# One 4 MB input load per half of the tokens, and a stashed residual read back from memory, in place of small input loads and a residual kept in SBUF

## The chip, the cores and the metric

The kernel runs on 8 cores of one Trainium2 chip. Each core computes its own share of the tokens, with no exchange between cores. The metric is the device time of the slowest core in microseconds (us).

## The reference

One "sandwich" layer over x of shape (4, 2048, 2048), in float32:

```python
x = feat_patch
# --- layer 0 (sandwich) ---
x = x + layernorm(mamba_like_block(layernorm(x)))      # the "attn" part
x = x + layernorm(ffn_with_moe(layernorm(x)))          # the "ffn" part
```

The attn part normalises again, projects 2048 channels to 96, applies a convolution of width 3, a selective scan over time with 16 states per channel, projects 96 back to 2048 and adds its own input:

```python
x = layer_norm(feat_patch, ln_w, ln_b)
x = x @ in_proj_W.T
...
y = ssm(x, x_proj_W, dt_proj_W, dt_proj_b, A_log, D_param)
out = y @ out_proj_W.T
return out + residual
```

The ffn part is a gated MLP of inner width 8192, plus a routed MLP of width 1024 that is scaled by the weights of a top-2 router.

## The kernel before, in words

**Layout.** A core owns 1024 tokens. The data lie transposed: 2048 channels as KC = 16 tiles of 128 partitions, tokens along the free dimension, worked through in halves of 512 (the loop variable is `hc`, the offset `off = 512 * hc`). A tile of 128 x 512 float32 has 256 KB. `x3` is the view of the core's input `xT` as (partition, tile, token).

**Stages in order of time.** The mixer (in-projection, convolution, scan; `xcb` holds the input as bf16, loaded by GpSimd's queue in chunks of 16 tiles x 512 tokens), then stage O (out-projection, residuals, two layer norms; from 443 to 786 us), the router, the routed MLP, the gate and up projections ("gu", 64 blocks), the down projection and the epilogue, which reads the stashed residual again.

**The order of the work.** Each engine runs its instructions in the order in which the program lists them. The class `Sched` gives each operation its semaphore waits: `reads`, `writes` and `waits` become waits for the tokens of earlier operations, a tile's resource (`Res`) holds its last writer and its readers. `S.dma("sync", ...)` issues a DMA from SP, `S.dma("scalar", ...)` from ScalarE's instruction stream (so a wait of such a DMA holds up ScalarE's later instructions), `S.dma("gpsimd", ...)` from GpSimd's. `S.fence()` makes the next instruction of every engine wait for all that was issued so far. `CW` is the list of the constants' loads, which nearly every TensorE operation waits for, too (they landed in the first 22 us).

**Stage O**, for each half `hc`, in this order:

1. *The out-projection loop* over 16 tiles `mc`. SP loads the tile of the input (L830, buffers `xld`, two of them). TensorE multiplies (L836, L838) into a bank of PSUM. VectorE multiplies the input tile by the row of reciprocal deviations (L844, `t_s`) and adds the bank (L847, `t_mr`) into `mr_sb`. ScalarE makes two casts of it, a copy and a square (L775, L777, in `stats_tile`), and TensorE sums them over the channels (L779, L784). TensorE runs in order, so the product of tile `mc + 1` stands behind the sums of tile `mc`.
2. *The rows*: seven small operations on 1 x 512 between ScalarE and VectorE (L793 to L805), and `bcast` (L811 on TensorE, L814 on ScalarE), which spreads a row over 128 partitions, into `bc_a` and `bc_b`.
3. *The residual loop* over 16 tiles `k`. SP loads the input tile again (L862, buffers `xld2`, two of them). VectorE multiplies in place (L866, `tx1`), GpSimd adds (L870, `tx2`), VectorE adds the input tile and writes the result to its own slice of `x2res` (L874, `tx3`). ScalarE issues the store of this tile to `x2_st` in HBM (L878) and makes the two casts (L885, L888); TensorE sums them (L891, L897).
4. *The rows again* (L906 to L922); the last operation is L922 (`tG`). The two results are kept in `rows4`. Then `bcast` twice.
5. *The normalising loop* over 16 tiles `k`: VectorE multiplies `x2res` by `bc_a` into `x2t` (L929, `tz1`, two buffers) and adds `bc_b` into `z4_sb` as bf16 (L932, `tz2`). `z4_sb` is what all later matmuls read.

After the second half the router's matmuls (L952) wait for the last L932.

**Memory.** SBUF is laid out by hand in regions B1, B2 and B3. `mr_sb` (32 KB per partition) lies in B1 over the mixer's tiles, `x2res` (32 KB) in the upper part of B2, `z4_sb` (32 KB) in B3 over `xcb`.

Of the kernel before, what the change touches and what calls it, by code (L numbers as in the profile page):

```python
# [206 lines left out]
def build_program(debug_taps=()):  # L207
# [112 lines left out]
    mr_sb = at("s_mr", (128, 16 * 512), F32, nc.lookup_mloc(xp_all.tensor).addr)  # L320
    assert (nc.lookup_mloc(rowsA.tensor).addr
            >= nc.lookup_mloc(mr_sb.tensor).addr + 32 * 1024), "mr overlaps rows"
    xld = [at(f"s_xld{i}", (128, 512), F32, RW0 + 2048 * i) for i in range(2)]
    xld2 = [at(f"s_xld2{i}", (128, 512), F32, WB0 + 2048 * i) for i in range(2)]
# [18 lines left out]
    sel8_sb = atb2("s_sel8", (8, 8 * 128), F32)  # L343
    cmb8 = atb2("s_cmb8", (8, 128), F32)
    lgt_sb = atb2("s_lgt", (8, 1024), F32)
    lgt_tm = atb2("s_lgttm", (128, 64), F32)
    rt_m1 = atb2("s_rtm1", (128, 8), F32)
    rt_t = atb2("s_rtt", (128, 8), F32)
    rt_t2 = atb2("s_rtt2", (128, 8), F32)
    comb_tm = atb2("s_combtm", (128, 8), F32)  # L350
    outTbf = atb2("s_outTb", (96, 2048), BF16)
    y_f = atb2("s_yf", (96, 1024), F32)
    y_bf = atb2("s_ybf", (96, 1024), BF16)
    rows4 = atb2("s_rows4", (1, 4 * 512), F32)
    cast_bf = [at(f"s_castb{i}", (128, 512), BF16, WB0 + 4096 + 1024 * i) for i in range(2)]
    cast_bf2 = [at(f"s_castb2{i}", (128, 512), BF16, WB0 + 6144 + 1024 * i) for i in range(2)]
    x2t = [at(f"s_x2t{i}", (128, 512), F32, WB0 + 8192 + 2048 * i) for i in range(2)]
    bc_b2 = at("s_bcb2", (128, 512), F32, WB0 + 12288)
    o2[0] = max(o2[0], B2 + 32 * 1024)
    M_SPILL0 = o2[0]  # L360
# [1014 lines left out]
```

How the kernel before makes its waits and increments, by code:

```python
        def run(e, emit=emit, wl=wl, inc=(inc_sem, inc_by), ph=ph, eng=eng):  # L66
            n0 = e.bass.n_instructions() if hasattr(e, "bass") else None
            for s, v in wl:
                e.wait_ge(_SEMS[s], v)
            inst = emit(e)
            inst.then_inc(_SEMS[inc[0]], inc[1])
            n1 = e.bass.n_instructions() if n0 is not None else None
            self.dbg_map[eng].append((n1 - n0 if n0 is not None else 1 + len(wl), ph))
# [133 lines left out]
def build_program(debug_taps=()):  # L207
# [1095 lines left out]
    final_waits = {}  # L1303
    for (s, v, _) in out_toks:
        final_waits[s] = max(final_waits.get(s, 0), v)
    fw = list(final_waits.items())
    def final_op(e, fw=fw):
        for s, v in fw:
            e.wait_ge(_SEMS[s], v)
        return e.nop()
    S.cnt["s_sy"] = S.cnt.get("s_sy", 0) + 1
    S.ops.append(("sync", lambda e: final_op(e).then_inc(_SEMS["s_sy"], 1)))
    with nc.Block() as block:
        @block.sync
```

## Time and profile before

| what | value |
|---|---|
| median of 3 runs | 2717.59 us (2714.5 to 2926.98) |
| the profiled execution's own time | 2718.68 us |
| its span (first to last instruction, core 2, the slowest) | 2717.1 us |
| spans of the 8 cores | 2701.4 to 2717.1 us |
| TensorE busy | 1920.2 us (71%) |
| VectorE, ScalarE, GpSimd busy | 394.6, 466.7, 355.5 us |
| stage O, from the fence to the last L932 | 443.3 to 785.6 us |
| router and routed MLP; gu; down; epilogue | to 1050; to 1940; to 2540; to the end |

The profile is of one execution on the slowest core, and its own time is 1.6 us over its span and 1.1 us over the median. Times are microseconds from the span's start; L12 is line 12 of the kernel. PE is TensorE (PEld its weight loads), DVE VectorE, ACT ScalarE, POOL GpSimd, SP SyncE; ACTq and SPq are the streams that issue DMAs. TensorE's granted clock is printed as a share of 2.4 GHz.

### The profile page before, as it was taken

To read this page: it belongs to the slowest core of one execution; us is meant where nothing else is said; L and a number is where in the kernel's file an instruction comes from. 1 tells how busy PE (TensorE), PEld (TensorE's weight loads), DVE (VectorE), ACT (ScalarE), POOL (GpSimd) and SP (SyncE) were. 2 spreads that over 40 slices of the span, in tenths; PEclk is the share of its full clock that TensorE was granted. 3 is DMA by queue.
4 is the path that set the end of the run, shared out by engine and by line. 5 is a ranking of instruction groups with operands and counts; after the bars stand their busy time and mean duration, and the time that the engine had idled before them with its cause. 6 is when DMAs were issued, how large, how long until landed. Compare 5 with 4: busy or idle time off the path is not lost.

```text
span 2717.1 us, 26955 instructions; the slowest of 8 cores (2701.4 to 2717.1 us)
## 1 busy us (share of the span) xinstructions
PE 1920.2 (71%) x7579; PEld 780.8 (29%) x7719; DVE 394.6 (15%) x589; ACT 466.7 (17%) x802; POOL 355.5 (13%) x400
## 2 busy tenths in 40 slices
PE   4444544434327967999999999999788898888200
PEld 2111110000003423444444444444333333333000
DVE  0553343253341100000000000000000000000222
ACT  3333211222311121111111111111100000000100
POOL 1000000020201201222222222222100000000122
PEclk8555555555558998999999999999899899999555
DMA  7220001131422354444444434344444334443233
GB/s 114 44 32 0 0 0 32 55 109 51 113 47 37 58 135 97 78 78 78 78 78 78 76 74 74 74 76 77 78 94 93 71 84 93 93 93 70 108 139 131
DMA packets 68011, 203.24 MB, mean 75 GB/s; under 512 B 7900, under 2 KB 18269, under 8 KB 63782
## 3 DMA queue, kind: packets, MB, share of 16 engines
q0 software_dynamic: 38608, 124.49, 26.4%
q1 hardware_dynamic: 15446, 35.07, 4.3%
q10 hardware_dynamic: 13824, 41.95, 4.2%
q8 instruction: 78, 1.28, 0.2%
q14 instruction: 55, 0.45, 0.1%
HBM read 292.41 MB, written 33.55 MB: 120 GB/s over the span
## 4 chain that ended last, share of the span: by engine, by line
PE 65%; DVE 11%; DMA 9%; issue 7%; ACT 4%; POOL 3%; DVEq 1%; SPq 0%; ACTq 0%; POOLq 0%
PE pb L1122 16%; PE pb L1131 16%; PE pb L1179 5%; PE pb L1176 4%; PE pb L1194 4%; PE pb L1191 4%; DMA s_epf<-f_stash 3%; DMA s_xld<-xT 2%; PE pb L1037 2%; PE pb L1046 2%; DVE s_xs L738 2%; PE pb L749 2%; DMA s_rdbuf<-Wrd 2%; POOL s_mr L870 1%; PE pb L1079 1%
## 5 line engine op out<-in xcount | busy, mean ns | idle before, releaser
L1122 PE MATMUL pb<-s_z,s_gbuf 128*128 128x512 bf16 x2007 | 461.5, 380 | 15.1 <-issue 12.9
L1131 PE MATMUL pb<-s_z,s_ubuf 128*128 128x512 bf16 x2007 | 459.9, 379 | 2.2
L1122 PEld LDWEIGHTS pb<-s_z,s_gbuf 128*128 128x128 bf16 x2048 | 200.8, 98 | 256.0 <-issue 15.6
L1131 PEld LDWEIGHTS pb<-s_z,s_ubuf 128*128 128x128 bf16 x2048 | 200.3, 98 | 241.7
L1208 DVE TENSOR_TENSOR s_fstg<-pb,s_frbuf 128x512 f32<-128x512 f32 x32 | 20.6, 686 | 1552.7 <-PE pb L1194 1552.7
L1143 POOL TENSOR_TENSOR s_h<-s_gs,s_us 128x512 bf16<-128x512 bf16 x128 | 147.1, 1150 | 678.6 <-ACT s_us L1140 678.6
L1176 PE MATMUL pb<-s_h,s_dbuf 128*128 128x512 bf16 x490 | 200.5, 409 | 18.0 <-issue 17.8
L1179 PE MATMUL pb<-s_h,s_dbuf 128*128 128x512 bf16 x512 | 208.7, 408 | 1.8 <-issue 0.4
L1194 PE MATMUL pb<-s_h,s_dbuf 128*128 128x512 bf16 x512 | 199.2, 389 | 1.1
L1191 PE MATMUL pb<-s_h,s_dbuf 128*128 128x512 bf16 x492 | 191.6, 389 | 4.1 <-PE pb L1179 4.1
L1137 ACT ACTIVATE s_gs<-pb 128x512 bf16<-128x512 f32 x128 | 76.5, 598 | 380.3 <-PE pb L1122 362.6
L1140 ACT ACTIVATE s_us<-pb 128x512 bf16<-128x512 f32 x128 | 76.5, 598 | 365.5 <-PE pb L1131 365.5
L870 POOL TENSOR_TENSOR s_mr<-s_mr,s_bcb 128x512 f32<-128x512 f32 x32 | 40.5, 1265 | 556.2 <-ACT s_bcb L814 501.3
L1216 ACT ACTIVATE s_fbf<-s_fstg 128x512 bf16<-128x512 f32 x32 | 20.1, 630 | 540.2 <-DVE s_fstg L1208 538.5
L749 PE MATMUL pb<-s_dA,s_selR 128*96 128x512 f32 x48 | 47.8, 1100 | 81.9 <-DVE s_dA L746 81.9
L1156 POOL DMA_DIRECT2D s_dbuf<-Wd x32 | 17.1, 533 | 529.3 <-PE pb L1179 314.7
L1079 PE MATMUL pb<-s_rh,s_rdbuf 128*128 128x512 bf16 x251 | 63.5, 410 | 30.7 <-DMA s_rdbuf<-Wrd 28.8
L1176 PEld LDWEIGHTS pb<-s_h,s_dbuf 128*128 128x128 bf16 x512 | 53.3, 104 | 93.2 <-issue 43.6
L779 PE MATMUL pb<-s_castb,s_o128b 128*1 128x512 bf16 x32 | 18.7, 584 | 77.2 <-ACT s_castb L775 77.2
L1179 PEld LDWEIGHTS pb<-s_h,s_dbuf 128*128 128x128 bf16 x512 | 53.0, 104 | 67.6 <-issue 18.0
L1191 PEld LDWEIGHTS pb<-s_h,s_dbuf 128*128 128x128 bf16 x512 | 51.0, 100 | 73.7 <-issue 26.0
L1194 PEld LDWEIGHTS pb<-s_h,s_dbuf 128*128 128x128 bf16 x512 | 51.0, 100 | 61.7 <-issue 13.7
(192 smaller groups left out, 1470.0 us busy)
## 6 DMA issues: line engine op xcount, KB each, us to landing
s_gbuf<-Wg POOLq DMA_DIRECT2D x64, 512.0 KB, 6.2
s_ubuf<-Wu POOLq DMA_DIRECT2D x64, 512.0 KB, 8.2
s_dbuf<-Wd POOLq DMA_DIRECT2D x32, 1024.0 KB, 9.0
s_xld<-xT SPq DMA_DIRECT2D x64, 256.0 KB, 2.9
s_xcb<-xT POOLq DMA_DIRECT2D x5, 2048.0 KB, 15.1
x_stash<-s_x2res ACTq DMA_DIRECT2D x32, 256.0 KB, 3.7
fr_stash<-s_frstg ACTq DMA_DIRECT2D x16, 512.0 KB, 5.7
s_frbuf<-fr_stash ACTq DMA_DIRECT2D x16, 512.0 KB, 8.7
```

The source lines that it names most:

```text
L749: tj8 = S.op("tensor", lambda e, j=j, jb=jb: e.matmul(pb[2][0:96, :], selR_sb[:, 96 * j:96 * (j + 1)], prod_b[jb][:], start=(j == 0), stop ...
L870: tx2 = S.op("gpsimd", lambda e, k=k: e.tensor_add(mr_sb[:, 512 * k:512 * (k + 1)], mr_sb[:, 512 * k:512 * (k + 1)], bc_b[:, :]), reads=[r ...
L1079: i = e.matmul(pb[bank][:, :], rdbuf[db][:, 128 * ikr:128 * (ikr + 1)], r_h_sb[:, 1024 * ikr + hof:1024 * ikr + hof + 512], start=(ikr == ...
L1122: i2 = e.matmul(pb[bg][:, :], gbuf[ib][:, 128 * k:128 * (k + 1)], z4_sb[:, 1024 * k + hof:1024 * k + hof + 512], start=(k == 0), stop=(k = ...
L1131: i2 = e.matmul(pb[bu][:, :], ubuf[ib][:, 128 * k:128 * (k + 1)], z4_sb[:, 1024 * k + hof:1024 * k + hof + 512], start=(k == 0), stop=(k = ...
L1137: tsl = S.op("scalar", lambda e, half=half, bg=bg: e.activation(gs_t[half][:], pb[bg][:, :], AF.Silu), reads=[r_pb[bg]], writes=[r_gs[half ...
L1140: tuc = S.op("scalar", lambda e, half=half, bu=bu: e.activation(us_t[half][:], pb[bu][:, :], AF.Copy), reads=[r_pb[bu]], writes=[r_us[half ...
L1143: S.op("gpsimd", lambda e, i=i, hof=hof, half=half: e.tensor_mul(h_all[:, 1024 * i + hof:1024 * i + hof + 512], gs_t[half][:], us_t[half][:]),
L1176: e.matmul(pb[b0][:, :], dbuf[0][:, 128 * ik:128 * (ik + 1)], h_all[:, 1024 * ik:1024 * ik + 512], start=(ik == 0), stop=False)
L1179: i2 = e.matmul(pb[b1][:, :], dbuf[0][:, 128 * ik:128 * (ik + 1)], h_all[:, 1024 * ik + 512:1024 * (ik + 1)], start=(ik == 0), stop=False)
L1191: e.matmul(pb[b0][:, :], dbuf[1][:, 128 * (ik - 32):128 * (ik - 31)], h_all[:, 1024 * ik:1024 * ik + 512], start=False, stop=(ik == NI - 1))
L1194: i2 = e.matmul(pb[b1][:, :], dbuf[1][:, 128 * (ik - 32):128 * (ik - 31)], h_all[:, 1024 * ik + 512:1024 * (ik + 1)], start=False, stop=(i ...
```

## The change

It replaces the way in which stage O gets its input tiles and keeps its result:

- One load of 16 tiles x 512 tokens (4 MB) per half, from SP, into a new `x_half`, at the top of the half. It replaces the 16 loads of L830 and the 16 of L862. `x_half` lies where `mr_sb` lay; `mr_sb` moves to B3, into the space of `z4_sb`. The second half's load writes what the first half's loops read, so it waits for their last reader.
- `x2res` is gone. The residual loop writes `x2t[k % 2]` and stores it to `x2_st` from there, so it also waits until the store and the casts of tile `k - 2` have read that buffer.
- Because `mr_sb` now lies over `z4_sb`, the normalising loops of both halves run after the second half's residual loop, behind a new `S.fence()`. They read each tile back from `x2_st` into `x2t[k % 3]` (three buffers), even tiles from ScalarE's stream, odd ones from SP's, and work in place.
- Small tiles get other addresses in B2.

The core of the diff:

```diff
+    x_half = at("s_xhalf", (128, 16 * 512), F32,
+                nc.lookup_mloc(xp_all.tensor).addr)
...
-    xld = [at(f"s_xld{i}", (128, 512), F32, RW0 + 2048 * i) for i in range(2)]
-    xld2 = [at(f"s_xld2{i}", (128, 512), F32, WB0 + 2048 * i) for i in range(2)]
...
+    x2t = [atb2(f"s_x2t{i}", (128, 512), F32) for i in range(3)]
+    mr_sb = at("s_mr", (128, 16 * 512), F32, B3)
-    x2res = at("s_x2res", (128, 16 * 512), F32, B2 + 32 * 1024)
...
     for hc in range(2):
         off = 512 * hc
+        t_xh = S.dma("sync", lambda e, off=off: e.dma_start(
+                         out=xh3[:, :, :], in_=x3[:, :, 1024 + off:1024 + off + 512]),
+                     writes=[r_xhalf])
         for mc in range(KC):
-            t_xl = S.dma("sync", lambda e, mc=mc, kk=kk, off=off: e.dma_start(
-                             out=xld[kk][:],
-                             in_=x3[:, mc, 1024 + off:1024 + off + 512]),
-                         writes=[r_xld[kk]])
...
         for k in range(KC):
             kk = k % 2
-            t_x2l = S.dma("sync", lambda e, k=k, kk=kk, off=off: e.dma_start(
-                              out=xld2[kk][:],
-                              in_=x3[:, k, 1024 + off:1024 + off + 512]),
-                          writes=[r_xld2[kk]])
...
             tx3 = S.op("vector", lambda e, k=k, kk=kk: e.tensor_add(
-                           x2res[:, 512 * k:512 * (k + 1)],
-                           mr_sb[:, 512 * k:512 * (k + 1)], xld2[kk][:]),
-                       reads=[r_mr, r_xld2[kk]], writes=[r_x2r[k]], waits=[tx2, t_x2l])
+                           x2t[kk][:], mr_sb[:, 512 * k:512 * (k + 1)],
+                           x_half[:, 512 * k:512 * (k + 1)]),
+                       reads=[r_mr, r_xhalf], writes=[r_x2t[kk]], waits=[tx2, t_xh])
...
-        t_r4b = bcast(bc_a, r_bca, row4(s_r4), r_rows4[s_r4], [tF], 3)
-        t_nm4b = bcast(bc_b, r_bcb, row4(s_nm4), r_rows4[s_nm4], [tG], 4)
+        ln4_toks.append((tF, tG))
+
+    S.fence()
+    for hc in range(2):
+        off = 512 * hc
+        s_r4, s_nm4 = 2 * hc, 2 * hc + 1
+        t_r4b = bcast(bc_a, r_bca, rows4[:, 512 * s_r4:512 * (s_r4 + 1)],
+                      r_rows4[s_r4], [ln4_toks[hc][0]], 3)
+        t_nm4b = bcast(bc_b, r_bcb, rows4[:, 512 * s_nm4:512 * (s_nm4 + 1)],
+                       r_rows4[s_nm4], [ln4_toks[hc][1]], 4)
         for k in range(KC):
-            kk = k % 2
-            tz1 = S.op("vector", lambda e, k=k, kk=kk: e.tensor_mul(
-                           x2t[kk][:], x2res[:, 512 * k:512 * (k + 1)], bc_a[:, :]),
-                       reads=[r_x2r[k], r_bca], writes=[r_x2t[kk]], waits=[t_r4b])
+            kk = k % 3
+            trl = S.dma("scalar" if k % 2 == 0 else "sync",
+                        lambda e, k=k, kk=kk, off=off: e.dma_start(
+                            out=x2t[kk][:], in_=x2_st[k, :, off:off + 512]),
+                        writes=[r_x2t[kk]], waits=[r_x2st[k]])
+            tz1 = S.op("vector", lambda e, kk=kk: e.tensor_mul(
+                           x2t[kk][:], x2t[kk][:], bc_a[:, :]),
+                       reads=[r_bca], writes=[r_x2t[kk]], waits=[trl, t_r4b])
```

The order on VectorE at the turn from the first half to the second, before (line numbers are those of each kernel; `s_rows_115` is `rows4`, `s_x2t` the two buffers, `s_z_144` is `z4_sb`):

```order
L874 TENSOR_TENSOR s_x2res<-s_mr,s_xld_95 128x512
L912 TENSOR_TENSOR s_rows<-s_rows 1x512
L914 TENSOR_TENSOR s_rows<-s_rows 1x512
L922 SCALAR_TENSOR_TENSOR s_rows_115<-s_rows,s_rows_115 1x512
L929 TENSOR_TENSOR s_x2t_120<-s_x2res,s_bca 128x512
L932 TENSOR_TENSOR s_z_144<-s_x2t_120,s_bcb 128x512
```

and the same place after the change:

```order
L862 TENSOR_TENSOR s_x2t_135<-s_mr,s_xhalf 128x512
L899 TENSOR_TENSOR s_rows<-s_rows 1x512
L901 TENSOR_TENSOR s_rows<-s_rows 1x512
L909 SCALAR_TENSOR_TENSOR s_rows_129<-s_rows,s_rows_129 1x512
L836 TENSOR_TENSOR s_bcb<-s_xhalf,s_bca 128x512
L839 TENSOR_TENSOR s_mr<-pb,s_bcb 128x512
```

The 32 instructions of the first half's normalising loop left this place; the second half's first product with `x_half` follows directly on the rows.

The order on ScalarE at the end of stage O, before (L957 is the router's):

```order
L906 ACTIVATE s_rows<-pb 1x512
L909 ACTIVATE s_rows<-pb 1x512
L916 ACTIVATE s_rows<-s_rows 1x512
L918 ACTIVATE s_rows_115<-s_rows 1x512
L814 ACTIVATE s_bca<-pb 128x512
L814 ACTIVATE s_bcb<-pb 128x512
L957 ACTIVATE s_lgt<-pb 8x512 x2
```

and after, up to the turn between the two normalising loops (`s_x2t_134`, `_135` and `_136` are the three buffers; the odd tiles' loads stand on SP):

```order
L905 ACTIVATE s_rows_129<-s_rows 1x512
L810 ACTIVATE s_bca<-pb 128x512
L810 ACTIVATE s_bcb<-pb 128x512
L925 DMA s_x2t_134<-x_stash 128x512
L925 DMA s_x2t_136<-x_stash 128x512
...
L925 DMA s_x2t_136<-x_stash 128x512
L810 ACTIVATE s_bca<-pb 128x512
L810 ACTIVATE s_bcb<-pb 128x512
L925 DMA s_x2t_134<-x_stash 128x512
L925 DMA s_x2t_136<-x_stash 128x512
```

ScalarE's eight loads of each half stand behind both of that half's broadcasts.

## Rows read from the trace of the kernel before

**Rows 1.** Busy time in one stretch, the first half's residual loop.

```profile
core 2: us, PE busy (x) PEld busy (x) DVE busy (x) ACT busy (x) POOL busy (x), PEclk, DMA share, GB/s
...
532.60:582.90 50.30, 18.39 (x31) 2.38 (x30) 22.16 (x32) 17.84 (x31) 20.23 (x16) 0.50 0.57 163
```

**Rows 2.** The chain that ended last, window 458 to 470: start, us, what.

```profile
458.90 2.43 DMA s_xld<-xT
...
461.34 0.58 PE pb L836
```

**Rows 3.** Timeline, tiles 13 and 15 of the first out-projection loop: start, us [idle before].

```profile
511.95 0.58 PE L836 MATMUL pb<-s_ybf,s_outTb 96*128 96x512 bf16 x1 [0.63 <-DMA s_xld<-xT]
...
522.07 0.58 PE L836 MATMUL pb<-s_ybf,s_outTb 96*128 96x512 bf16 x1 [0.64 <-PE pb L784]
```

**Rows 4.** Waits in window 425:790: us in total, times, longest.

```profile
DVE s_mr L847 <- PE pb L838: 114.1, 30, 4.1
...
DVE s_x2res L874 <- POOL s_mr L870: 50.6, 32, 2.5
```

**Rows 5.** Timeline at the start of stage O.

```profile
442.53 0.63 ACT L764 ACTIVATE s_ybf<-s_yf 96x512 bf16<-96x512 f32 x1 [5.97 <-DVE s_yf L760]
443.33 36.01 SPq L830 DMA_DIRECT2D s_xld<-xT  x10
...
443.51 2.04 PE L811 MATMUL pb<-s_r1own,s_o1x 1*128 1x512 f32 x2 [1.93 <-ACT s_ybf L764]
...
446.51 0.69 DVE L844 TENSOR_TENSOR s_bcb<-s_xld,s_bca 128x512 f32<-128x512 f32 x1 [4.08 <-DMA s_xld<-xT]
```

**Rows 6.** DMA in 443:447, 40 slices of 0.1 us: the first two 256 KB loads.

```profile
GB/s 0 0 0 0 0 0 0 0 0 0 0 0 0 143 102 82 143 225 143 369 389 369 369 389 410 369 369 389 410 307 226 21 20 0 0 0 0 0 0 0
```

**Rows 7.** DMA in 55:75, 0.5 us slices: one load of `xcb`, bytes written.

```profile
GB/s 0 0 0 0 0 0 0 0 0 0 0 4 66 57 147 207 205 199 199 207 203 213 207 205 211 207 203 172 188 195 166 184 152 115 156 113 25 8 0 0
```

**Rows 8.** DMA to landing: all `xcb` loads; L830 alone; L862 alone; L878's stores; the epilogue's reads of the stash.

```profile
DMA to landing us min/median/max: 14.8/15.1/32.0
...
DMA to landing us min/median/max: 2.5/2.6/3.9
...
DMA to landing us min/median/max: 2.7/3.5/5.0
...
DMA to landing us min/median/max: 2.0/3.7/5.2
...
DMA to landing us min/median/max: 4.4/4.8/6.6
```

**Rows 9.** Timeline, from the first residual loop to the second half.

```profile
582.16 0.69 DVE L874 TENSOR_TENSOR s_x2res<-s_mr,s_xld 128x512 f32<-128x512 f32 x1 [1.51 <-POOL s_mr L870]
...
588.92 0.68 DVE L922 SCALAR_TENSOR_TENSOR s_rows<-s_rows,s_rows 1x512 f32<-1x512 f32 x1 [1.55 <-ACT s_rows L918]
...
594.34 0.68 DVE L929 TENSOR_TENSOR s_x2t<-s_x2res,s_bca 128x512 f32<-128x512 f32 x1
...
595.12 0.69 DVE L932 TENSOR_TENSOR s_z<-s_x2t,s_bcb 128x512 bf16<-128x512 f32 x1
595.73 0.69 DVE L929 TENSOR_TENSOR s_x2t<-s_x2res,s_bca 128x512 f32<-128x512 f32 x1
...
615.54 0.69 DVE L844 TENSOR_TENSOR s_bcb<-s_xld,s_bca 128x512 f32<-128x512 f32 x1
```

**Rows 10.** Timeline, end of stage O.

```profile
759.10 0.68 DVE L922 SCALAR_TENSOR_TENSOR s_rows<-s_rows,s_rows 1x512 f32<-1x512 f32 x1 [1.54 <-ACT s_rows L918]
759.25 3.75 PE L811 MATMUL pb<-s_rows,s_o1x 1*128 1x512 f32 x4 [3.23 <-ACT s_rows L918]
...
763.15 0.60 ACT L814 ACTIVATE s_bcb<-pb 128x512 f32<-128x512 f32 x1 [1.16 <-PE pb L811]
...
784.91 0.69 DVE L932 TENSOR_TENSOR s_z<-s_x2t,s_bcb 128x512 bf16<-128x512 f32 x1
785.96 6.01 PE L952 MATMUL pb<-s_z,s_routerTb 128*8 128x512 bf16 x16 [22.96 <-DVE s_z L932]
```

More of the change, by code:

```diff
@@ L319, in build_program @@
                   nc.lookup_mloc(dA_b[0].tensor).addr)
[L320 removed]
+    x_half = at("s_xhalf", (128, 16 * 512), F32,
+                nc.lookup_mloc(xp_all.tensor).addr)
     assert (nc.lookup_mloc(rowsA.tensor).addr
[L322 to L324 removed]
+            >= nc.lookup_mloc(x_half.tensor).addr + 32 * 1024), "x_half overlaps rows"
     rh_tmp = at("s_rhtmp", (128, 1024), BF16, B1)
@@ L342, in build_program @@
     routerTbf = atb2("s_routerTb", (128, 128), BF16)
[L343 to L360, printed above, removed]
     xprojTbf = atb2("s_xprojTb", (96, 38), BF16)
@@ L379, in build_program @@
     selR_sb = atb2("s_selR", (128, 12 * 96), F32)
+    y_f = atb2("s_yf", (96, 1024), F32)
+    y_bf = atb2("s_ybf", (96, 1024), BF16)
+    lgt_sb = atb2("s_lgt", (8, 1024), F32)
+    lgt_tm = atb2("s_lgttm", (128, 64), F32)
+    rt_m1 = atb2("s_rtm1", (128, 8), F32)
+    rt_t = atb2("s_rtt", (128, 8), F32)
+    rt_t2 = atb2("s_rtt2", (128, 8), F32)
+    rows4 = atb2("s_rows4", (1, 4 * 512), F32)
+    cast_bf = [atb2(f"s_castb{i}", (128, 512), BF16) for i in range(2)]
+    cast_bf2 = [atb2(f"s_castb2{i}", (128, 512), BF16) for i in range(2)]
+    x2t = [atb2(f"s_x2t{i}", (128, 512), F32) for i in range(3)]
+    bc_b2 = atb2("s_bcb2", (128, 512), F32)
+    comb_tm = atb2("s_combtm", (128, 8), F32)
     B3 = B2 + 64 * 1024
@@ L843, in build_program @@
             r_bcb_i = r_bcb if mc % 2 == 0 else r_bcb2
-            t_s = S.op("vector", lambda e, kk=kk, bcb_i=bcb_i: e.tensor_mul(
-                           bcb_i[:, :], xld[kk][:], bc_a[:, :]),
-                       reads=[r_xld[kk], r_bca], writes=[r_bcb_i], waits=[t_xl, t_r1b])
+            t_s = S.op("vector", lambda e, mc=mc, bcb_i=bcb_i: e.tensor_mul(
+                           bcb_i[:, :], x_half[:, 512 * mc:512 * (mc + 1)], bc_a[:, :]),
+                       reads=[r_xhalf, r_bca], writes=[r_bcb_i], waits=[t_xh, t_r1b])
             t_mr = S.op("vector", lambda e, mc=mc, bank=bank, bcb_i=bcb_i: e.tensor_add(
@@ L874, in build_program @@
             tx3 = S.op("vector", lambda e, k=k, kk=kk: e.tensor_add(
[L875 to L882 removed]
+                           x2t[kk][:], mr_sb[:, 512 * k:512 * (k + 1)],
+                           x_half[:, 512 * k:512 * (k + 1)]),
+                       reads=[r_mr, r_xhalf], writes=[r_x2t[kk]], waits=[tx2, t_xh])
+            tst = S.dma("scalar", lambda e, k=k, kk=kk, off=off: e.dma_start(
+                            out=x2_st[k, :, off:off + 512], in_=x2t[kk][:]),
+                        reads=[r_x2t[kk]], waits=[tx3])
+            r_x2st[k] = tst if hc == 0 else tst
             cb4 = cast_bf if k % 2 == 0 else cast_bf2
             rc4 = r_cast if k % 2 == 0 else r_cast2
[L885 to L890 removed]
+            tca = S.op("scalar", lambda e, kk=kk, cb4=cb4: e.activation(
+                           cb4[0][:], x2t[kk][:], AF.Copy),
+                       reads=[r_x2t[kk]], writes=[rc4[0]], waits=[tx3])
+            tcb = S.op("scalar", lambda e, kk=kk, cb4=cb4: e.activation(
+                           cb4[1][:], x2t[kk][:], AF.Square),
+                       reads=[r_x2t[kk]], writes=[rc4[1]], waits=[tx3])
             ts1 = S.op("tensor", lambda e, k=k, cb4=cb4: e.matmul(
```

22 lines of the change are left out of this document (5 added, 17 removed).

## The prediction

> **What bounds the kernel now.** I read the page first: TensorE is busy 71% of the span, and the change touches none of the stages where it is. Stage O, from 443.3 to 785.6 us, is the only place it touches, so all views were read there. In it TensorE's granted clock is 0.50 (1.2 GHz) and DVE is busy less than half of the residual loop: 22.16 of 50.30 us [rows 1]. No engine is full there; each loop runs at the length of a chain of small operations.
>
> In the out-projection loop the waits show a circle: DVE's L847 waits for TensorE's L838 in 30 of 32 cases, 114.1 us in total [rows 4]; it releases ScalarE's cast, and that TensorE's sums, behind which the next product stands. One turn takes (522.07 - 511.95) / 2 = 5.06 us [rows 3]. The chain view tells something else: it runs through the load of `xld`, 2.43 us in each turn, which ends just as L836 starts [rows 2]. This is the place to doubt. At tile 13 L836 starts after 0.63 us idle, put down to the load; at tile 15, when this loop has no load left to wait for, the idle time is 0.64 us and the turn no shorter [rows 3]. L836 reads no `xld`, and the load lands in that gap by coincidence. So I take the small loads as hidden, apart from the first.
>
> In the residual loop DVE waits for GpSimd in all 32 cases [rows 4]; its turn is 50.3 / 16 = 3.14 us [rows 1] and does not depend on the load of L862 either. The normalising loop is DVE alone: 1.40 us a tile ((784.91 - 763.15 - 0.77) / 15, from the first L932 just behind the broadcast) [rows 10], the same as from one L929 to the next, 595.73 - 594.34 = 1.39 [rows 9].
>
> **Part A, the first 4 MB load.** Before, the first product L844 starts at 446.51, 3.18 us after SP's first issue [rows 5]. After, it waits until the whole of `x_half` has landed. No row shows a 4 MB load on SP's queue. Two things are near: the two first `xld` loads began to move at 444.3, 1.0 us after the issue, and from 444.9 on ran at 369 to 410 GB/s, so that they count as started at 1.5 us [rows 5, 6]; and a load of `xcb`, which reads the same 4 MB with the same runs of 2 KB, takes 14.8 us at least, 15.1 at the median and 32.0 at most [rows 8], moving data for about 12.5 us [rows 7] (it writes bf16, so what is read is double the 205 GB/s shown). From below: 1.5 + 4.19 MB / 410 GB/s + 0.3 for the end = 12.0 us. From above: 32.0 us, when two such loads and the constants ran at once. The value I take is 14.0 us, just below the quiet `xcb` load, since SP's loads start moving a little sooner. L844 then starts at 443.33 + 14.0 + 0.1 = 457.4: **+10.9 us**. Nothing hides it; only one broadcast stands beside it.
>
> The row first: the two loads ran at 369 to 410 GB/s, with all cores at work [rows 6]. The Trainium skill (DMA: Bandwidth & Descriptors, Anatomy of one DMA) gives 2.0 us plus bytes / 436 GB/s, which would be 11.6 us for 4 MB, and the sum below would be 4.8 us smaller; its section Bandwidth puts about 358 GB/s per core when both cores of an HBM domain stream, so 13.7 us by the same form. I stay with the rows.
>
> **Part B, the turn between the halves.** The second load can go out when the last L874 has read `x_half`: 582.16 + 0.69 + 0.08 = 582.93 [rows 9]; it lands at 596.9. Beside it run the rows up to 588.92 + 0.68 = 589.6, so some 7.3 us stay open. L844 starts at 597.0 instead of 615.54 [rows 9], because the 32 normalising instructions are no longer between: **-18.5 us**. From there to the last L922 nothing is changed.
>
> The residual loop gets a new wait: `tx3` of tile k must wait for the store of tile k-2. Two turns are 6.28 us, less its own 0.69; the store lands after 3.7 us, 5.2 at most [rows 8], so even the slowest has 0.3 us to spare. Queued behind a late `tx3` would be DVE's next `tx1`, then GpSimd and the casts. Cost 0, at most 1 us. The casts read the buffer within 2 us and don't matter. The new addresses I cost at nothing.
>
> **Part C, the normalising loops at the end.** Before, from the end of the last L922 (759.78) to the end of the last L932 (785.60) there are 25.8 us [rows 10]. After:
> - The fence holds TensorE's broadcast until L922 is done. At the fence ahead of stage O it starts 443.51 - 443.16 = 0.35 us after the last operation [rows 5]: 760.13 instead of 759.25. `bc_b` is then ready 0.88 us later than now, at 764.63 [rows 10].
> - ScalarE's loads stand behind this broadcast. Tile 0 is issued at 764.73. Its landing time: 2.5 to 3.9 us for quiet loads of this size, median 2.6, 3.5 beside stores; 4.4 to 6.6 for the double size in the epilogue [rows 8]. I take 2.8, near the quiet ones, because no store runs by then but two loads overlap. First product at 767.61.
> - Each buffer goes round in 0.78 + 0.69 (L929 start to L932 end [rows 9]) + 0.08 + 2.8 + 0.08 = 4.43 us, for three buffers 1.48 us a tile, against 1.40 of DVE. So the loads bound it, barely. First half's end: 767.61 + 15 x 1.48 + 1.47 = 791.28.
> - At the turn tile 0 needs `bc_b`'s broadcast (0.17 + 0.60), the issue (0.10) and a landing (2.88), bare: 795.03. Second half's end: 818.70.
>
> That is 818.70 - 785.60 = **+33.1 us**. The first half's loop came back (22.4), and 10.7 are added by the fence, the two bare landings and the longer turn. The router follows as before.
>
> **The sum.** +10.9 - 18.5 + 33.1 = +25.5 us. The profiled execution took 2718.68 us, so 2744.2; against the median of the runs, 1.1 us lower, 2743.1. I say 2743.5. The bytes moved are about the same: 64 loads of 256 KB before, 2 of 4 MB and 32 of 256 KB after. No stage after 786 us is touched; two runs of before differ by 3 us.
>
> **The rivals.**
> 1. *The chain view is right, and the small loads did set the turn.* For it: rows 2, in nearly every turn. Then with the input in SBUF each of 32 turns of the out-projection loop loses the load's part. L836 could start when L784 is through, 0.63 us earlier [rows 3]: -20.2 us, and a sum of +5 us, 2724. For the end to come out not slower than before, the turn would have to lose over 25.5 / 32 = 0.8 us; if it fell by the whole 2.43 us of the load it would be -78, and 2666, faster by 1.9%. Against it: tiles 13 to 15, and that the wait is named at an instruction which doesn't read the tile.
> 2. *The 4 MB load is slow.* Place: the top of each half, and it counts twice, since the second one is bare beyond 7 us. Every us over 14.0 costs 2. At the longest `xcb` landing, 32.0 us [rows 8], it is +36, so 2780, slower by 2.3%; from 28.5 us on it is over 2%. For it: all cores start it at the same moment, and the queue's longest loads in the trace are far smaller. Against it: the quiet `xcb` loads are made at the same moment on all cores too and take 15.
> 3. *The reloads are slow.* With 3.5 us a landing the tile takes 1.71 us, +8.3 in all, 2752; with 4.8, 2.14 us, +24, so 2768. For it: each waits for a buffer, so nothing averages it out. Against it: 256 KB per 1.48 us are 177 GB/s, less than half of what rows 6 show.
> 4. *The reloads cost nothing.* With 2.6 us a landing or less DVE's 1.40 us is the bound: -3, 2741.
>
> **How the numbers follow.** My own case with rival 4: 0.70. Rival 3: 0.12, mostly its near end. Rival 2: 0.10, most of it at 18 to 24 us, 2751 to 2763; over 28.5 us 0.03. Rival 1: 0.08, of which 0.02 for a gain over 2%. My case alone spans 2737 (load 12.0 us, turn 1.40) to 2750. The range for 8 in 10 goes from 2736 to 2762. 2% (54 us) is about what a measurement of this kernel can tell from no change: faster 0.02, same 0.93, slower 0.05 (rival 2 at its far end, or 2 and 3 together).
>
> **What would show it.** In the profile after: the first L836 (the old L844) some 14 us after SP's issue; that DVE instruction again some 14 us after the last `tx3` of the first half; turns of 5.06 and 3.14 us unchanged; two runs of 16 products with `x2t` at 1.4 to 1.5 us a tile; the last one some 25 us later than 785.6. I am wrong if the out-projection turn is shorter than 4.9 us, if `x_half` lands after more than 18 us, if `tx3` waits for a store, or if the stages after the router take another time than now.

## The result, and the profile after

The changed kernel takes 2750.91 us at the median of 10 runs (2743.08 to 2996.43); the kernel before, run beside it, 2715.57 us (2713.88 to 2926.98). The ratio is 1.0126, with a 95% interval of 1.0109 to 1.0143, so 34.2 us longer (29.6 to 38.8). The forecast was 2743.5 us in a range of 2736 to 2762, and "within 2%": the time lies in the range and in that case, but the sum of +25.5 us was 9 us short. The disturbed runs at the upper ends are left out of this ratio and all that follow, though not out of the medians.

The profiled execution after the change took 2751.17 us. The spans of the cores after the change (us from first to last instruction, mean granted clock of TensorE):

```profile
core 0: 2732.7 us, clock 0.806
...
core 2: 2733.9 us, clock 0.805
...
core 4: 2749.6 us, clock 0.804
...
die 0 (median of its cores): 2737.1 us, clock 0.806
die 1 (median of its cores): 2738.3 us, clock 0.806
```

The two dies agree in span and clock, but the single cores differ by 17 us. I had read the trace of before on core 2 alone; after the change core 4 is the slowest. So the table is a mean over the eight cores, each read from its own timeline. "To first product" runs from SP's first issue in stage O to the first product of the input tile (the old L844); "first half, rest" goes on to the start of the half's last row operation, L922 (now L909); the two columns after it are counted from the end of such an operation, so its own 0.7 us stands in none of the four, but in stage O; the last column is all that stands behind stage O. Us:

| kernel | to first product | first half, rest | first half's end to second half's end | from there to the last L932 (L931) | stage O | behind it |
|---|---|---|---|---|---|---|
| before | 3.2 | 142.4 | 170.2 | 25.8 | 342.3 | 1921.0 |
| after | 16.1 | 142.4 | 154.1 | 61.2 | 374.6 | 1917.8 |
| forecast of the difference | +10.9 | 0 | -18.5 | +33.1 | +25.5 | 0 |
| measured difference (before rounding) | +12.9 | +0.1 | -16.0 | +35.4 | +32.4 | -3.2 |

Each of the three parts has the sign and nearly the size that was forecast, and each was 2.0 to 2.5 us too favourable. What lies behind stage O is not longer; that it is 3.2 us shorter says little, since there the eight cores of the kernel before alone differ by 18 us (1913.1 to 1931.5). By core, stage O grew by 28.2 us (core 2) to 35.9 (core 1).

The loads and the stores on core 4, in the view of the DMA issues (output and input, queue, count, KB each, median us from issue to landing):

```profile
s_xhalf<-xT SPq DMA_DIRECT2D x2, 4096.0 KB, 17.0
x_stash<-s_x2t ACTq DMA_DIRECT2D x32, 256.0 KB, 2.0
...
s_x2t<-x_stash SPq DMA_DIRECT2D x16, 256.0 KB, 2.9
s_x2t<-x_stash ACTq DMA_DIRECT2D x16, 256.0 KB, 3.0
```

The 4 MB load takes 17.0 us here where 14.0 were forecast (the trace has one landing of the two, that of the first load); a reload takes 2.9 to 3.0 where 2.8 were. The stores land in 2.0 us, against 3.7 before [rows 8], when loads ran beside them, so `tx3` had 1.7 us more to spare than was reckoned.

The waits on core 4 in the window 425:850 (who waits for whom: us in total, times, longest):

```profile
DVE s_mr L839 <- PE pb L830: 113.4, 30, 4.1
...
DVE s_x2t L862 <- POOL s_mr L858: 50.9, 32, 2.5
...
DVE s_bcb L836 <- DMA s_xhalf<-xT: 30.1, 2, 18.4
...
DVE s_x2t L928 <- DMA s_x2t<-x_stash: 13.6, 9, 7.9
```

The first two answer to [rows 4] and have not moved (114.1 and 50.6 before): the loops wait for the same things as long as ever. The third is new, two waits and 30.1 us: it is what the large load leaves open at the top of each half. The fourth is the bare landing behind the fence (7.9 us), the one at the turn between the two normalising loops (3.4) and small gaps beside them. VectorE waits for a store nowhere in this window, so the new wait of the residual loop cost nothing.

The timeline of core 4 from the start of stage O to its end (start, us, engine, line, what, and in brackets the idle time before and what ended it):

```profile
445.94 0.40 SPq L820 DMA_DIRECT2D s_xhalf<-xT  x1
...
463.44 0.69 DVE L836 TENSOR_TENSOR s_bcb<-s_xhalf,s_bca 128x512 f32<-128x512 f32 x1 [18.41 <-DMA s_xhalf<-xT]
...
599.06 0.69 DVE L862 TENSOR_TENSOR s_x2t<-s_mr,s_xhalf 128x512 f32<-128x512 f32 x1 [1.51 <-POOL s_mr L858]
599.83 0.38 SPq L820 DMA_DIRECT2D s_xhalf<-xT  x1
...
605.87 0.68 DVE L909 SCALAR_TENSOR_TENSOR s_rows<-s_rows,s_rows 1x512 f32<-1x512 f32 x1 [1.55 <-ACT s_rows L905]
...
618.26 0.69 DVE L836 TENSOR_TENSOR s_bcb<-s_xhalf,s_bca 128x512 f32<-128x512 f32 x1 [11.71 <-DMA s_xhalf<-xT]
...
760.95 0.68 DVE L909 SCALAR_TENSOR_TENSOR s_rows<-s_rows,s_rows 1x512 f32<-1x512 f32 x1 [1.54 <-ACT s_rows L905]
761.99 7.16 PE L807 MATMUL pb<-s_rows,s_o1x 1*128 1x512 f32 x8 [4.12 <-DVE s_rows L909]
...
769.52 0.69 DVE L928 TENSOR_TENSOR s_x2t<-s_x2t,s_bca 128x512 f32<-128x512 f32 x1 [7.90 <-DMA s_x2t<-x_stash]
...
793.97 0.69 DVE L931 TENSOR_TENSOR s_z<-s_x2t,s_bcb 128x512 bf16<-128x512 f32 x1
...
798.04 0.69 DVE L928 TENSOR_TENSOR s_x2t<-s_x2t,s_bca 128x512 f32<-128x512 f32 x1 [3.39 <-DMA s_x2t<-x_stash]
...
821.82 0.69 DVE L931 TENSOR_TENSOR s_z<-s_x2t,s_bcb 128x512 bf16<-128x512 f32 x1
822.87 3.57 PE L950 MATMUL pb<-s_z,s_routerTb 128*8 128x512 bf16 x8 [53.72 <-DVE s_z L931]
```

It is read as pairs. The first product waits from the issue at 445.94 to 463.44. The second load goes out 0.08 us after the last read of `x_half` (599.06 + 0.69 = 599.75), and the next product comes 18.43 us after that issue; of these the rows hide some 6.7 us (to 605.87 + 0.68), and 11.71 are bare. From the end of the second half's rows (760.95 + 0.68 = 761.63) it is 7.89 us to the first normalising product, from there 25.14 to the end of the first loop's last L931, 3.38 to the next product and 24.47 to the end of the last L931, 822.51. The router (L950) follows 0.36 us later, as before [rows 10].

### The profile page after: what moved, and what is told of

Its sections match the earlier page's. It is cut to its first block, busy times and chain, and to the rows that moved or that the text cites. A ratio compares the mean times of both kernels' runs of the same rounds, so it can differ in the third digit from the quotient of the medians.

```text
span 2749.6 us, 26926 instructions; the slowest of 8 cores (2732.7 to 2749.6 us)
## 1 busy us (share of the span) xinstructions
PE 1913.5 (70%) x7579; PEld 779.6 (28%) x7719; DVE 396.2 (14%) x589; ACT 466.2 (17%) x802; POOL 355.5 (13%) x400
## 4 chain that ended last, share of the span: by engine, by line
PE 65%; DVE 11%; DMA 9%; issue 7%; ACT 4%; POOL 3%; DVEq 0%; SPq 0%; ACTq 0%; POOLq 0%
PE pb L1120 16%; PE pb L1129 16%; PE pb L1177 5%; PE pb L1174 4%; PE pb L1192 4%; PE pb L1189 4%; DMA s_epf<-f_stash 3%; PE pb L1035 2%; PE pb L1044 2%; DVE s_xs L734 2%; PE pb L745 2%; DMA s_rdbuf<-Wrd 2%; POOL s_mr L858 1%; PE pb L1077 1%; DMA s_xhalf<-xT 1%
## 5 line engine op out<-in xcount | busy, mean ns | idle before, releaser
L1174 PE MATMUL pb<-s_h,s_dbuf 128*128 128x512 bf16 x490 | 201.2, 411 | 15.6 <-issue 15.2
L1177 PE MATMUL pb<-s_h,s_dbuf 128*128 128x512 bf16 x512 | 209.4, 409 | 1.8 <-issue 0.4
L1192 PE MATMUL pb<-s_h,s_dbuf 128*128 128x512 bf16 x512 | 194.0, 379 | 1.1
L1189 PE MATMUL pb<-s_h,s_dbuf 128*128 128x512 bf16 x492 | 186.4, 379 | 4.2 <-PE pb L1177 4.2
L1189 PEld LDWEIGHTS pb<-s_h,s_dbuf 128*128 128x128 bf16 x512 | 50.0, 98 | 70.2 <-issue 11.6
```

The lines of the kernel that those rows point to most:

```text
L1174: e.matmul(pb[b0][:, :], dbuf[0][:, 128 * ik:128 * (ik + 1)], h_all[:, 1024 * ik:1024 * ik + 512], start=(ik == 0), stop=False)
L1177: i2 = e.matmul(pb[b1][:, :], dbuf[0][:, 128 * ik:128 * (ik + 1)], h_all[:, 1024 * ik + 512:1024 * (ik + 1)], start=(ik == 0), stop=False)
L1189: e.matmul(pb[b0][:, :], dbuf[1][:, 128 * (ik - 32):128 * (ik - 31)], h_all[:, 1024 * ik:1024 * ik + 512], start=False, stop=(ik == NI - 1))
L1192: i2 = e.matmul(pb[b1][:, :], dbuf[1][:, 128 * (ik - 32):128 * (ik - 31)], h_all[:, 1024 * ik + 512:1024 * (ik + 1)], start=False, stop=(i ...
```

## The experiments

Nine kernels ran, one of them twice. e1, e2 and e3 each take away one part of what the change brought; e4 and e6 put parts of it into the kernel before; e5 cuts the large load of the changed kernel in two; e7 (run again as e7b), e8 and e9 shorten the loops' turns themselves. Each ratio is to the kernel before, run beside it in the same series; the medians of different series are not to be compared (the kernel before had 2715.6, 2730.1, 2719.3 and 2733.2 us in the four); stage O and its stretches are means over the eight cores of the profiled execution.

### The input by tiles instead of in one load (e1)

`x_half` stays, but is filled by 16 loads of 256 KB, each with its own resource, so that the product of tile `m` waits for tile `m` alone.

```diff
-        t_xh = S.dma("sync", lambda e, off=off: e.dma_start(
-                         out=xh3[:, :, :], in_=x3[:, :, 1024 + off:1024 + off + 512]),
-                     writes=[r_xhalf])
+        for m in range(KC):
+            t_xh[m] = S.dma("sync", lambda e, m=m, off=off: e.dma_start(
+                                out=x_half[:, 512 * m:512 * (m + 1)],
+                                in_=x3[:, m, 1024 + off:1024 + off + 512]),
+                            writes=[r_xh[m]])
```

> The changed kernel with x_half loaded as 16 loads of 256 KB with their own waits instead of one of 4 MB. My theory: the first product starts about 3.2 us after the first issue (16.1 on average over the cores now), -13 us; in the second half it follows the rows at once, -9 us (16.1 us of landing less the 7 us of rows beside it). So some 22 us less than the changed kernel, 2729. Rival (the loads' bytes cost time however they are cut, by contention with the stores): under 10 us less, with stores that land in 3.7 us again and tx3 waiting for them.

Measured: ratio 1.0015 (0.9988 to 1.0042), median 2725.31 us; stage O 350.7 us against 374.6. The first product came after 3.3 us (16.1 in after), and from one half's end to the other's it took 143.3 us (154.1). That is (before rounding) 12.9 and 10.9, together 23.7 of the 24.0 us: the size of the load was paid twice, the second time less what the rows hide. The transfer itself got no shorter: the last of the first half's 16 loads lands 17.5 to 20.0 us (by core) after the first issue, and the one large load took 13.8 to 17.0. What the cut buys is that the first tile is there after 2.8 us. What is left against before, 350.7 - 342.3 = 8.4 us, is the price of the reloads and the two loops at the end.

### All reloads from SP (e2)

```diff
-            trl = S.dma("scalar" if k % 2 == 0 else "sync",
+            trl = S.dma("sync",
```

> The changed kernel with all reloads of x2_st issued by SP instead of even ones by ScalarE. My theory: load 0 goes out at the fence and lands under the broadcasts; the first product starts with bc_a's end, some 4.8 us earlier (about 3.2 instead of 8.1 us after the last row); the turn between the two loops stays bare (buffer 0 is read by tile 15), about 3.1 us; 1.54 us a tile unchanged. So -4.8 us. Rival (one queue cannot keep three loads going): a tile over 1.7 us, so no gain or a loss of up to 5 us.

Measured: ratio 1.0103 (1.0046 to 1.016), median 2743.06 us; stage O 370.7 us, 3.9 less than after; 3.5 of it are in the end (57.8 us instead of 61.2), where 4.8 were expected. The timeline of core 4 behind the fence:

```profile
755.04 15.99 SPq L925 DMA_DIRECT2D s_x2t<-x_stash  x10
...
757.40 0.60 ACT L810 ACTIVATE s_bca<-pb 128x512 f32<-128x512 f32 x1 [3.33 <-DMA s_x2t<-x_stash]
...
759.16 0.69 DVE L928 TENSOR_TENSOR s_x2t<-s_x2t,s_bca 128x512 f32<-128x512 f32 x1 [4.30 <-DMA s_x2t<-x_stash]
```

SP issues tile 0 at 755.04, before ScalarE copies the broadcast row out of PSUM at 757.40, and not behind it. The gap ahead of the first product falls from 8.15 to 3.72 us (mean of the cores). A tile then takes 1.637 us in the first half, more than the 1.562 of the changed kernel, and that gives 1.1 us of it back. So the price of queueing a load behind a broadcast on ScalarE, some 4 us, is shown.

### Six buffers for the reloads (e3)

```diff
-    x2t = [atb2(f"s_x2t{i}", (128, 512), F32) for i in range(3)]
+    x2t = [atb2(f"s_x2t{i}", (128, 512), F32) for i in range(6)]
...
-            kk = k % 3
+            kk = k % 6
```

> The changed kernel with six buffers for x2t in the reload loops instead of three. My theory: the loop of 1.54 us a tile is one third of a buffer's round trip; with six buffers DVE's 1.40 us bounds it: -4.3 us over both halves, the turn between them stays as it is because ScalarE's loads stand behind the broadcasts. Rival (bandwidth or landing beside other loads bounds the loop): still 1.5 us or more a tile and landings well over 3 us.

Measured: ratio 1.008 (1.0047 to 1.0113), median 2747.53 us; stage O 369.5 us, of which the end, 57.4 us, is 3.9 less than in after. VectorE's products on the slowest core's timeline:

```profile
771.50 0.69 DVE L928 TENSOR_TENSOR s_x2t<-s_x2t,s_bca 128x512 f32<-128x512 f32 x1 [9.89 <-DMA s_x2t<-x_stash]
...
772.90 0.68 DVE L928 TENSOR_TENSOR s_x2t<-s_x2t,s_bca 128x512 f32<-128x512 f32 x1
...
774.30 0.68 DVE L928 TENSOR_TENSOR s_x2t<-s_x2t,s_bca 128x512 f32<-128x512 f32 x1
```

They stand 1.40 us apart with no wait, which is VectorE's own pace as in [rows 9]. With three buffers the round trip of a buffer set the pace, as the forecast had it. But the gap at the turn between the loops grew from 3.29 to 4.20 us. The load that is waited for there is issued 0.28 us behind the last L931 in both kernels, but lands after 3.8 us (mean of the cores) where it took 2.9 with three buffers. With six buffers more loads are out at once at this place; that they slow each other down was not taken apart.

### The 4 MB load put into the kernel before (e4)

The normalising loop stays where it was. `x_half` lies where `mr_sb` lay, `mr_sb` in the place of `x2res`, and `tx3` writes in place.

```diff
-    mr_sb = at("s_mr", (128, 16 * 512), F32, nc.lookup_mloc(xp_all.tensor).addr)
+    x_half = at("s_xhalf", (128, 16 * 512), F32,
+                nc.lookup_mloc(xp_all.tensor).addr)
-    x2res = at("s_x2res", (128, 16 * 512), F32, B2 + 32 * 1024)
+    mr_sb = at("s_mr", (128, 16 * 512), F32, B2 + 32 * 1024)
+    x2res = mr_sb
...
+        t_xh = S.dma("sync", lambda e, off=off: e.dma_start(
+                         out=xh3[:, :, :], in_=x3[:, :, 1024 + off:1024 + off + 512]),
+                     writes=[r_xhalf])
```

> The kernel before, with the 4 MB load per half, but the residual kept in SBUF (tx3 writes in place into mr_sb, no x2res), no reloads, no fence, the normalising loop inside its half. My theory (the time is the bare landing of each 4 MB load plus the end loops): only the first landing is bare, 14 to 17.5 us instead of 3.2, since the second load lands under the 22 us of the normalising loop. So +11 to +14 us over the kernel before, 2727 to 2730, and from the first L922-like row to the end of stage O nothing longer than before. Rival (the added time sits in stages after O, or a 4 MB load disturbs the loops too): 2735 to 2750, or stage O longer by over 16 us.

Measured: ratio 1.0026 (1.0004 to 1.0049), so +7 us (+1 to +13), median 2729.53 us; stage O +13.2 us by its stages, 12.8 of them ahead of the first product, which is at the upper edge of what the ratio allows, and within the +11 to +14 that were expected. Of the waits of VectorE for the load there is one on the slowest core, in the window 430:800:

```profile
DVE s_bcb L843 <- DMA s_xhalf<-xT: 18.1, 1, 18.1
```

The second load costs nothing here: from one half's end to the other's it took 170.1 us, as in before. The normalising loop that the change moved away had been the cover of the second load. That is why the load counts twice after the change and once here.

### The load on two queues (e5)

```diff
-        t_xh = S.dma("sync", lambda e, off=off: e.dma_start(
-                         out=xh3[:, :, :], in_=x3[:, :, 1024 + off:1024 + off + 512]),
-                     writes=[r_xhalf])
+        t_xh0 = S.dma("sync", lambda e, off=off: e.dma_start(
+                          out=xh3[:, 0:8, :], in_=x3[:, 0:8, 1024 + off:1024 + off + 512]),
+                      writes=[r_xhalf])
+        t_xh = S.dma("scalar", lambda e, off=off: e.dma_start(
+                         out=xh3[:, 8:16, :], in_=x3[:, 8:16, 1024 + off:1024 + off + 512]),
+                     writes=[r_xhalf2])
```

The first product waits for both halves.

> The changed kernel with the 4 MB load cut into two of 2 MB, tiles 0 to 7 issued by SP and 8 to 15 by ScalarE at the same time; all products wait for both. Theory bandwidth (the memory or the 16 DMA engines set the 14 to 17 us): the first product still starts 14.5 to 17.5 us after the first issue on the cores. Rival (one queue's descriptors set it): it starts after 9 to 11 us, and stage O gets 12 us shorter.

One execution: 2747.47 us, stage O 374.5 us, the first product after 16.7 us (13.9 to 18.3 by core; in after 16.1). The view of the tile `x_half` on core 0 of this kernel (operation, count, duration of the issue in ns, first and last start in us):

```profile
L821 SPq DMA_DIRECT2D s_xhalf<-xT x2: 375/388/402, 446.9 to 601.2; - x2
L824 ACTq DMA_DIRECT2D s_xhalf<-xT x2: 391/428/466, 446.9 to 606.7; - x2
...
DMA to landing us min/median/max: 12.6/16.6/17.6
```

Both issues of the first half start at 446.9, and at 2 MB each the loads still take up to 17.6 us side by side: a second queue buys nothing, so what holds the transfer is shared by both queues; which part of the path it is, no run shows. (In the second half ScalarE's part goes out 5.5 us late, 606.7 against 601.2, since it stands behind the rows in ScalarE's stream; so only the first half is the comparison that was wanted.)

### The tile loads and half the input bytes in the kernel before (e6)

e4 with the tile loads of e1, whose edits are shown above. The input is read once a half and not twice, and all else stays as before.

> As e4_inplace_big, but x_half loaded in 16 loads with their own waits. My theory: no term of the change is left (no bare landing, no reload, no fence), so stage O takes 342 us as in the kernel before, and the time is that of the kernel before within noise; half the bytes of the input loads of stage O are gone and buy nothing, as the small loads were hidden. Rival (the chain view was right, the two loads per tile set the loops' turns): stage O shorter by 10 to 20 us.

Measured: ratio 1.0011 (0.9982 to 1.0039), median 2718.29 us; stage O 342.9 us, before 342.3. The four stretches of the table (3.4, 143.0, 170.1 and 25.8) agree with before within 0.6 us. That half of the input's loads are gone is worth nothing, and the small loads are not in either turn. This is the direct answer to the rival that believed the chain of waits.

### Shorter turns (e7, and the same kernel again as e7b)

The true bound of the out-projection loop is the circle of [rows 4]: the next product stands on TensorE behind this tile's sums. e7 is e6 with the product of tile `mc + 1` issued ahead of the sums of tile `mc`, and with `tx1` of tile `k + 1` between `tx2` and `tx3` of tile `k`.

```diff
+        emit_op1(0)
         for mc in range(KC):
+            if mc + 1 < KC:
+                emit_op1(mc + 1)
+            t_op = t_ops[mc]
...
+        tx1n = emit_tx1(0)
...
-            tx1 = S.op("vector", lambda e, k=k: e.tensor_mul(
+            tx1 = tx1n
...
+            if k + 1 < KC:
+                tx1n = emit_tx1(k + 1)
```

> e6_inplace_tiles with another order of the same operations: TensorE gets the product of tile mc+1 ahead of the sums of tile mc, and VectorE the multiplication tx1 of tile k+1 ahead of the addition tx3 of tile k. My theory (the turns are circles of waits through engines that run in order): the out-projection turn falls from 5.03 to about 3.3 us, the residual turn from 3.07 to about 2.1; stage O shorter by 32 x 1.7 + 32 x 1.0 = 86 us, 2630. Rival (the turns are set by work that is there in any order, semaphore waits on TensorE above all): under 30 us less.

> e7_pipelined once more, for its ratio to the kernel before: 0.969 (2631 over 2716), from the 83 us that stage O got shorter in its profile.

Measured: ratio 0.9677 (0.9636 to 0.9718), median 2635.39 us; stage O 259.1 us in both, 83.8 less than e6. The profiled executions took 2632.78 and 2636.02 us; the ratio is that of e7b. TensorE's first instruction of each tile in e7b, core 2:

```profile
472.15 0.58 PE L839 MATMUL pb<-s_ybf,s_outTb 96*128 96x512 bf16 x1 [0.76 <-ACT s_castb L775]
...
475.44 0.58 PE L839 MATMUL pb<-s_ybf,s_outTb 96*128 96x512 bf16 x1 [0.69 <-ACT s_castb L777]
...
478.65 0.59 PE L839 MATMUL pb<-s_ybf,s_outTb 96*128 96x512 bf16 x1 [0.64 <-ACT s_castb L777]
```

and the same instruction of the kernel after the change, core 2:

```profile
467.91 0.59 PE L828 MATMUL pb<-s_ybf,s_outTb 96*128 96x512 bf16 x1 [0.63 <-PE pb L780]
...
472.94 0.58 PE L828 MATMUL pb<-s_ybf,s_outTb 96*128 96x512 bf16 x1 [0.63 <-PE pb L780]
```

The turn is 5.03 us after the change, 5.06 before [rows 3] (over twelve turns and all cores 5.05 in both), and 3.2 to 3.3 in e7b. So the order of the instructions set it, with the input in SBUF or not. The residual loop's turn fell from 3.11 us in e6 to 2.24. The two reorderings were not run one by one; by these turns some 54 of the 84 us come from the first and 26 from the second.

### The same order in the kernel before (e8) and in the changed one (e9)

The edit of e7 alone, made once in the kernel before and once in the changed one; in both `tx1` of the next tile moves up as here:

```diff
+            if k + 1 < KC:
+                tx1n = emit_tx1(k + 1)
             tx3 = S.op("vector", lambda e, k=k, kk=kk: e.tensor_add(
```

> The kernel before with that same new order alone; its small loads stay, two buffers each. My theory: a load lands 2.6 to 3.6 us after its issue, a buffer goes round in about 4.5 us, so 2.3 us a tile would still be covered: about the same time as e7_pipelined, within 10 us. Rival (with shorter turns the small loads become the bound): slower than e7_pipelined by over 15 us, and DVE waits for xld or xld2 in most turns.

> The changed kernel with the new order alone. If the terms of the change are independent of the loops' turns: the loops take what they take in e7_pipelined (no small loads), the turn between the halves is 154 - 42 = 112 us from tg0 to tg1, the end loops 61 us, so stage O takes 16.1 + 101 + 112 + 61 + 1 = 291 us, 32 over e7_pipelined, and the whole 2663. Rival (the new wait of tx3 for a store of two tiles before, with turns of 2 us, becomes the bound now): the residual turns longer by 0.5 us or more, stage O over 300 us and DVE's tx3 waiting for DMA x_stash.

e8: ratio 0.9741 (0.9717 to 0.9766), median 2648.72 us, stage O 271.3 us. It is 12.1 us longer than e7b, and the two ratios are 17 us apart, where at most 10 were expected. The waits of e8, core 2, in the window 430:740, say why:

```profile
DVE s_x2res L891 <- DMA s_xld<-xT: 16.9, 18, 1.8
...
DVE s_bcb L853 <- DMA s_xld<-xT: 5.3, 3, 4.1
```

With short turns two buffers for the small loads no longer cover them: VectorE waits for the residual loop's loads 18 times in 32 turns (15 to 22 by core). (The name in such a row is that of the last to come; here an experiment stands beside it, e7b, in which these loads are out of the loop and so are 12 us. e7b also reads the input once and not twice; buffers and bytes were not taken apart.) The loads of the kernel before were hidden because the turns were long. My theory is out, and the rival nearly as written: VectorE waits in over half of the residual turns, while the cost is 17 us by the ratios and 12 in stage O.

e9: ratio 0.9804 (0.9762 to 0.9847), median 2669.51 us where 2663 were expected, stage O 293.9 us where 291 were. The waits in the same window, core 2:

```profile
DVE s_bcb L845 <- DMA s_xhalf<-xT: 29.9, 2, 18.7
...
DVE s_x2t L879 <- DMA x_stash<-s_x2t: 1.1, 1, 1.1
```

The two waits for the 4 MB load are as long as in the changed kernel (30.1 us on core 4). Stage O is 34.7 us over e7b's, where it is 32.4 over before's in the original order: the three terms of the change hardly depend on the turns. Against e8, the kernel before in the new order, it is only 22.6 us longer, because the change also takes away the small loads that e8 now waits for: what was hidden and worth nothing at the long turns is worth some 12 us at the short ones. With the residual loop's turn cut from 3.09 to 2.27 us the new wait for a store shows up for the first time, once on each core in this window and 0.7 to 1.2 us long: the margin that was reckoned in the forecast is used up at this turn.

## Why the prediction was right, and where it fell short

**The bound.** Right. The loops are bound by their circles of small operations and not by the small loads: the first half's stretch is 142.4 us before and after (the forecast had the residual turn as 3.14 us from one window; from L874 to L874, and L862 to L862 after the change, it is 3.09 in both), e6 agrees with before, and e7 shortens it by 41 us with a change of order alone. The rival that believed the chain of waits (-20.2 us) is ruled out. It was tiles 13 to 15 [rows 3], where the same idle time stood with no load left to wait for, that gave it away beforehand.

**Part A.** The mechanism was right, the size off: +12.9 us instead of +10.9. The step that failed is "the value I take is 14.0 us". The landing of the 4 MB load by core, 0 to 7, is 14.0, 16.4, 13.8, 16.0, 17.0, 15.7, 15.2 and 16.8 us, at the mean 15.6. The product starts 0.5 us behind the landing (on core 4 445.94 + 17.0 = 462.94, product at 463.44), not 0.1. I had taken the value from the `xcb` loads of core 2, and core 2 is the one on which they are the fastest. In the view of the line that loads `xcb`, core 6 of the kernel before has for the same kind of load:

```profile
DMA to landing us min/median/max: 17.8/18.5/33.8
```

Over the eight cores the medians of `xcb` lie between 15.1 and 18.5 us, at the mean 16.7. On core 2 itself the load landed after 13.8 us, 0.2 us from the forecast. The metric is the slowest core, so a landing had to be read on all of them. The lower bound of 12.0 us was built on a rate that two small loads reached on core 2; the forecast says "with all cores at work", which [rows 6] don't show, and core 4 moved its 4 MB at 4.19 MB / (17.0 - 1.5) us = 270 GB/s, not at 369 to 410. With 15.6 + 0.5 the term is 16.1 - 3.2 = +12.9.

The Trainium skill's form (DMA: Bandwidth & Descriptors, Anatomy of one DMA), which the page fits for DMAs that GpSimd issues, and by which the load would land after 11.6 us, is not met here: no core landed it in less than 13.8 in this profile, and the mean is 15.6.

**Part B.** -16.0 us instead of -18.5, and the failed step is the same one: "it lands at 596.9", 14.0 us after the issue, with 7.3 us open. Its cover was right: the rows hide 606.55 - 599.83 = 6.7 us on core 4, and 589.6 - 582.93 = 6.7 were forecast. But from issue to product it took 15.9 (core 0) to 18.4 us (core 4), 17.5 at the mean where 14.1 were forecast, and VectorE's bare wait is 10.8 us at the mean, 3.5 more than forecast; e1, which takes the large loads out, gives 10.9. The second load is so 1.4 us slower than the first (16.1 from issue to product); its landing is not in the trace, and why it is slower stays open. Some 0.9 us came back at a place that I had put down as unchanged: from the second half's first product to its L909 it takes 760.95 - 618.26 = 142.69 us, where before it was 759.10 - 615.54 = 143.56 [rows 9, 10]; e1 has 142.7 too, e4 and e6 143.5, so it goes with the normalising loop that left, and its cause was not looked for. The new wait of the residual loop cost 0 as forecast, with more room than reckoned, since the stores landed in 2.0 us.

**Part C.** +35.4 us instead of +33.1. By its steps, mean of the cores:

| step | forecast | measured |
|---|---|---|
| end of L909 to the first product | 7.83 | 8.15 |
| a tile, first half | 1.48 | 1.562 |
| last L931 of the first half to the next product | 3.75 | 3.29 |
| a tile, second half | 1.48 | 1.560 |

The tile is the term that was too small: 30 x 0.08 = 2.4 us. A landing of 2.94 us (mean of the 192 in the trace) instead of 2.8 gives 0.14 / 3 = 0.05 us a tile of it. Another 0.08 / 3 = 0.03 is that the product starts 0.16 us behind the landing of its load, where the forecast put 0.08. The first gap is 0.3 longer: tile 0 is issued after 4.49 us (4.95 forecast) and lands in 2.80, as forecast, but the product starts only 0.85 us behind the landing; why it is so much here, nothing shows. The turn is 0.5 shorter, since the load goes out 0.28 us behind the last L931 and not 0.87: on core 4 ScalarE's copy into `bc_b` starts at 794.81 and takes 0.60 us, and the load behind it in the same stream is issued at 794.93, while the copy runs. The forecast had it wait for the copy's end. 2.4 + 0.3 - 0.5 is the 2.2 us that were missing. e3 shows that the buffers bound the tile, e2 that the loads behind the broadcast made the first gap. The rival of slow reloads had only its near end (its nearest case was 3.5 us a landing), and the one that they cost nothing is out.

**The sum.** A was 2.0 us too low, B 2.5 and C 2.3, and with the small stretch between, stage O came to +32.4 and not +25.5. The ratio gives +34.2 (29.6 to 38.8), which holds the 32.4. The spans of the slowest cores differ by 32.5 (2717.1 and 2749.6), the means over the cores by 29.3, since there the 3.2 us behind stage O are taken off. That all three parts erred to the same side means that the time within the range owes something to luck: my own case ended at 2750, and the result lies at its edge. The width of the range, put there mostly for the 4 MB load, was what held it.

## What to carry to other kernels

One large load costs its landing, less the work that stands beside it, at each use of its buffer: here 12.9 us at the first and 10.9 at the second, and nothing at the second in e4. A load by tiles into the same buffer cost one tile's landing. Before a loop is moved, look what it hid: here the normalising loop was the cover of the next half's load. When the chain of waits names a DMA at an instruction that doesn't read it, compare a turn in which that transfer is missing, and look for the order of the instructions that sets the turn: here it was worth 84 us, and the loads nothing until it was mended.
